# One ring of six PSUM banks for both kinds of attention scores, and another order of TensorE's work in each step

## The reference, cut to what matters

```
q = (x @ wq), k = (x @ wk), v = (x @ wv)          # split in heads
scores = einsum('bhqd,bhkd->bhqk', q, k) / sqrt(hd)
scores = where(causal, scores, min)
attn = softmax(scores, axis=-1)
ctx = einsum('bhqk,bhkd->bhqd', attn, v)
return ctx @ wo + bo
```

## Time and profile before

| | us |
|---|---|
| median of three runs (2633.34 to 2634.40) | 2634.18 |
| the profiled execution, its own time | 2634.95 |
| its span, first to last instruction | 2633.3 |
| attention, TensorE's first to last matmul in it (298.7 to 959.1) | 660 |
| PE busy / DVE / ACT / POOL over the span | 2435.7 / 1221.1 / 818.4 / 903.7 |

### The profile page before, as it was taken

One profiled execution on the slowest core, in us unless ns is written; L12 is line 12 of the kernel. 1 busy time (PEld: TensorE's weight loads), 2 busy tenths in 40 slices (PEclk: granted clock), 3 DMA queues, 4 the chain that ended last, 5 costly groups with the idle time before them and its releaser, 6 DMA issues. The chain is left out here.

```text
span 2633.3 us, 39827 instructions
## 1 busy us (share of the span) xinstructions
PE 2435.7 (92%) x12833; PEld 1800.0 (68%) x12833; DVE 1221.1 (46%) x2498; ACT 818.4 (31%) x1371; POOL 903.7 (34%) x1092
## 2 busy tenths in 40 slices
PE   7999699999999968599999996899999979999997
PEld 5888455555555536478888885688888768888886
DVE  3333477777777749701211113767766371111121
ACT  3222055555555541044444442101101112222221
POOL 0000155555555535323333333516243122222211
PEclk9999699999999988899999998899999989999999
DMA  6665735455445335410101102221312051000000
GB/s 246 225 223 193 182 84 135 108 120 132 108 120 132 77 111 176 157 40 17 64 32 63 62 19 84 96 94 66 110 49 96 31 191 40 32 32 32 32 33 32
DMA packets 154489, 255.29 MB, mean 97 GB/s; under 512 B 9648, under 2 KB 47536, under 8 KB 153904
## 3 DMA queue, kind: packets, MB, share of 16 engines
q1 hardware_dynamic: 137712, 208.20, 26.5%
q0 software_dynamic: 6144, 25.17, 2.9%
q10 hardware_dynamic: 10560, 20.97, 2.3%
HBM read 161.50 MB, written 92.27 MB: 96 GB/s over the span
## 5 line engine op out<-in xcount | busy, mean ns | idle before, releaser
L737 DVE CUSTOM_DVE_ANT_0 p_junk<-psum,p_causal 128x896 bf16<-128x896 f32 (+7 forms) x512 | 370.6, 752 | 159.8 <-PE psum L597 149.8
L700 ACT ACTIVATE p_probs<-psum 128x512 f32<-128x512 f32 (+1 forms) x640 | 331.3, 554 | 325.9 <-PE psum L608 320.6
L1149 POOL TENSOR_TENSOR p_h_lo<-p_h,p_h_hi 128x512 fp32r<-128x512 f32 x128 | 165.1, 1290 | 338.3 <-ACT p_h_hi L1178 338.3
L608 PE MATMUL psum<-p_qst,p_kst 98*128 98x512 f32 (+3 forms) x768 | 246.0, 384 | 17.2 <-ACT p_probs L700 10.9
L608 PEld LDWEIGHTS psum<-p_qst,p_kst 98*128 98x128 f32 x768 | 131.4, 190 | 170.8 <-ACT p_probs L700 84.8
L520 POOL TENSOR_SCALAR_AFFINE_SELECT p_probs<-p_probs 128x128 f32<-128x128 f32 x512 | 146.0, 306 | 264.8 <-ACT p_probs L700 263.8
L597 PE MATMUL psum<-p_kst,p_qst 96*128 96x512 f32 (+5 forms) x768 | 205.8, 369 | 20.8 <-DMA p_kst<-k_parts 17.3
L1802 POOL CAST p_h<-p_h 128x512 fp32r<-128x512 f16 x128 | 92.6, 723 | 373.1 <-ACT p_h L1826 373.1
L846 PE MATMUL psum<-p_xT_hi,tern 128*128 128x512 f32 x512 | 206.4, 403 | 1.4 <-DVE p_xT_lo L1248 1.4
L1217 PE MATMUL psum<-tern,p_h_hi 128*128 128x512 f32 x512 | 203.0, 397 | 2.1 <-POOL p_h_lo L1149 2.1
L846 PE MATMUL psum<-p_xT,p_w_hi 128*128 128x512 f32 x512 | 204.0, 398 | 0.7 <-ACT p_xT L1813 0.7
(11 more groups left out here) (184 smaller groups left out, 4639.8 us busy)
## 6 DMA issues: line engine op xcount, KB each, us to landing
p_qst<-q_parts SPq DMA_DIRECT2D x96, 256.0 KB, 4.5
p_kst<-k_parts SPq DMA_DIRECT2D x96, 256.0 KB, 6.8
q_parts<-p_qk_out SPq DMA_DIRECT2D x32, 512.0 KB, 2.8
k_parts<-p_qk_out SPq DMA_DIRECT2D x32, 512.0 KB, 2.7
ffn_x<-x SPq DMA_DIRECT2D x12, 1024.0 KB, 5.6
p_x<-in_x_t POOLq DMA_DIRECT2D x8, 1024.0 KB, 6.4
p_raw<-in_f_w POOLq DMA_DIRECT2D x8, 1024.0 KB, 8.0
v_rows<-p_v_out SPq DMA_DIRECT2D x32, 256.0 KB, 4.9
```

The lines of the kernel that those rows point to most:

```text
L608: mm = pe.matmul(ST_BANKS[st % 2][:, col:col + CH - q0], kst[s][0:KD + 2, g, j * P:(j + 1) * P], qst[s][0:KD + 2, c, g, q0:CH], start=True ...
L700: act.activation(probs[:, n % 2, g, col:CH], ST_BANKS[st % 2][:, col:CH], ACT.Exp, scale=SM_SCALE).then_inc(p_ready, 1)
L737: dve.tensor_tensor_reduce(halves_of(junk[:, which, 0:n]), scores, halves_of(causal[:, SEQ - n:SEQ]), 1.0, FLOOR, ALU.add, ALU.max, rowmax ...
L1149: pool.tensor_tensor(h_lo[:, m % 2, :], h[:, m % 2, :], f32(h_hi[:, m % 2, :]), ALU.subtract).then_inc(hl_done, 1)
```

## The change

All second and first scores take their banks from one ring of six (banks 0 to 5) in the order in which TensorE computes them. A long entry takes two adjoining banks (one is skipped at the ring's end). Each access waits for whoever used its bank last: for the exponential (`p_ready`) if that was a second score, for the maximum (`s_used`) if it was an entry. The ring is computed once for all units (`ring`), and the program checks that every unit of the same parity sees the same pattern. In the last unit, whose entries are left out, their banks stay reserved in the count, but nobody waits for them. The words of `STEPS` change as well. Two start values of semaphores are set by GpSimd where the semaphore is made and no longer by VectorE.

```diff
-    STEPS = [([(0, 0)], "seeesseeevose"), ([(0, 1), (0, 3)], "eesseseesvo"), ([(0, 2)], "sseeseseevoe"),
-             ([(1, 0)], "ssesesvo"), ([(1, 1)], "seesvosesee"), ([(1, 2)], "ssvsso"), ([(1, 3)], "sessesevo"),
-             ([(1, 4)], "sseessvo"), ([(1, 5), (1, 7)], "sseessvo"), ([(1, 6)], "sseessvo")]
+    STEPS = [([(0, 0)], "seseeseeeeseevo"), ([(0, 1), (0, 3)], "sesessevo"),
+             ([(0, 2)], "eeesssvos"), ([(1, 0)], "esesssevo"),
+             ([(1, 1)], "ssesveseo"), ([(1, 2)], "sssveeseo"),
+             ([(1, 3)], "sseessvo"), ([(1, 4)], "sesseveseo"),
+             ([(1, 5), (1, 7)], "ssessevo"), ([(1, 6)], "ssessevo")]
...
-        S_RING = 4
-        ST_BANKS = [psum[:, 4, :], psum[:, 5, :]]
...
+        N_BANKS = 6
...
         def ring():
...
+            taken, user, at = {}, {}, 0
+
+            def take(key, n):
+                nonlocal at
+                at += n == 2 and at % N_BANKS == N_BANKS - 1
+                taken[key] = [((at + k) % N_BANKS, user.get((at + k) % N_BANKS)) for k in range(n)]
+                at += n
+
+            def used(key):
+                for bank, _ in taken[key]:
+                    user[bank] = key
...
+            for u in range(NU):
+                at += -at % N_BANKS if u % 2 == 0 else 0
+                k = head = 0
+                for _, order in STEPS:
+                    for what in order:
+                        if what == "s":
+                            take(("s", u, head), 1)
+                            used(("s", u, head))
+                            head += 1
+                        elif what == "e":
+                            take(("e", u, k), n_banks(ROUND[k]))
+                            if u < NU - 1 or k == turned(1):
+                                used(("e", u, k))
+                            k += 1
+            return taken
...
+                def before(u, s, kind, n):
...
+                        if who == "e":
+                            out.append((bank, s_used, S_RING + (m if not steady and unit < 0 else LEAD + PER_ROUND * v + (0 if not steady and unit == NU - 1 else m)) + 1))
+                        else:
+                            out.append((bank, p_ready, 2 + ST_PER_UNIT * v + m + 1))
+                    return out
...
-                    for half, (bank, back) in enumerate(banks):
+                    for half, (bank, free, value) in enumerate(banks):
                         k0 = half * keys
-                        pe.wait_ge(s_used, S_RING + at - back + 1)
+                        if free is not None:
+                            pe.wait_ge(free, value)
...
-                    pe.wait_ge(p_ready, ST_PER_UNIT * u + st + 1)
+                    (bank, free, value), = before(u, s, "s", st)
+                    pe.wait_ge(free, value)
                     for c, j, q0, col in blocks_of(n):
-                        mm = pe.matmul(ST_BANKS[st % 2][:, col:col + CH - q0], kst[s][0:KD + 2, g, j * P:(j + 1) * P],
+                        mm = pe.matmul(psum[:, bank, col:col + CH - q0], kst[s][0:KD + 2, g, j * P:(j + 1) * P],
```

More of the change, by code:

```diff
@@ new lines, in used @@
+            def used(key):
+                for bank, _ in taken[key]:
+                    user[bank] = key
+            for k, e in enumerate(FIRST_ROUND):
+                take(("e", -1, k), n_banks(e))
+                used(("e", -1, k))
+            for u in range(NU):
[12 more added lines that the diff above has]
+                            k += 1
@@ new lines, in ring, with seen_from @@
+            return taken
+        RING = ring()
+        def seen_from(u, kind, n):
+            return [(bank, prev and (prev[0], prev[1] - u, prev[2])) for bank, prev in RING[kind, u, n]]
+        for u in range(NU - 2):
+            for n in range(ST_PER_UNIT):
+                assert (u == 0 and n < HPG) or seen_from(u, "s", n) == seen_from(2 + u % 2, "s", n)
+            for k in range(PER_ROUND):
+                assert (u == 0 and k < STEPS[0][1].count("e")) or seen_from(u, "e", k) == seen_from(2 + u % 2, "e", k)
@@ L434, in phase_attention, with banks_of @@
+        def banks_of(s, kind, n):
+            return [bank for bank, _ in RING[kind, 2 + s, n]]
         entries_in = lambda text: text.count("e")
@@ L581, in _, with score_entry @@
             def _(pe):
-                def score_entry(at, banks, e, u, s):
+                def before(u, s, kind, n):
+                    steady = not isinstance(u, int)
+                    out = []
+                    for bank, prev in RING[kind, 2 + s if steady else u, n]:
+                        if prev is None:
+                            out.append((bank, None, 0))
+                            continue
+                        who, unit, m = prev
+                        v = u + (unit - 2 - s) if steady else unit
+                        if who == "e":
[3 more added lines that the diff above has]
+                    return out
+                def score_entry(banks, e, u, s):
                     ahead, c, tile, g = e
@@ L586, in score_entry @@
                     if tile is None:
-                        (bank, back), = banks
-                        pe.wait_ge(s_used, S_RING + at - back + 1)
+                        (bank, free, value), = banks
+                        pe.wait_ge(free, value)
                         pe.wait_ge(nm_ready, 2 * (u + ahead) + c + 1)
@@ L706, in body @@
                     steps = pair_steps(i, last)
-                    for n, (u, _, step) in enumerate(steps[:2 * N_STEPS]):
+                    for n, (u, s, step) in enumerate(steps[:2 * N_STEPS]):
                         if n + 1 < len(steps):
@@ L775, in normalize_between @@
                         if part < PARTS - 1:
-                            entries(around, first + part, first + part + 1)
+                            entries(around, s, first + part, first + part + 1)
                 for k, e in enumerate(FIRST_ROUND):
-                    maximum(k, lead_banks[k], k % 2, e, -1)
-                entries(0, 0, TO[1])
+                    maximum(k, [bank for bank, _ in RING["e", -1, k]], k % 2, e, -1)
+                entries(0, 0, 0, TO[1])
                 def body(i, last):
```

48 lines of the change are left out of this document (21 added, 27 removed).

## The result

| | us |
|---|---|
| before, median (2633.34 to 2635.98) | 2634.29 |
| after, median of 4 runs (2612.50 to 2615.57) | 2614.65 |
| after, 5 more runs (2613.12 to 2615.77) | 2614.20 |
| ratio to before, 95% interval | 0.9924 [0.9906, 0.9941] |

What follows compares the result with a forecast made beforehand. It took attention to be bound by TensorE, with waits mostly on banks ScalarE still reads. 2634.95 - 14 (units) - 7.5 (last unit) = 2613.5; the median is 0.8 lower, so 2613 us, 80% range 2590 to 2641.

Steps and rivals of the forecast that it cites:

- Waits of a unit: In each attention unit on TensorE: waits fall from 2.9 to 1.3 us; with splits, 15 x 0.95 = 14 us less.
- splits: Steps where `v` and `o` are parted: 0.3 us a split, three instead of one, +0.6 us a unit, +10 us.
- Step 0: First step of a unit: an entry and the transpose wait for second scores' banks, 0.7 us in all.
- the small waits in the other steps: Outside steps 0 and 6: no bank waits but no room; some 0.5 us of small excesses beside short matmuls.
- Step 6: Its first second score waits for VectorE's maximum behind the product: 0.6 us taken, between 0.3 and 0.75.
- the product would end with GpSimd's first tensor-tensor: VectorE's product before step 6: by the shared-port rule it ends with that operation, wait 0.3 us, total 2609.
- The last unit: Attention's unit without entries: of 9.3 us of waits about 1.1 stay, two splits cost 0.6, so 7.5 us less.
- The head: Start of attention: the load of the turned maxima sets the first second score; 0 taken, with -1.5 to +1.
- The second scores wait for VectorE: Rival: the product stands over GpSimd's second tensor-tensor, step 6 waits 2.3 us more a unit; 2647, slower; chance 0.13.
- the clock stays what it is: TensorE in attention: its clock is unchanged, since nothing lets it idle; no time given to it.
- As many waits as before: Rival: waits move to VectorE's queue in place of ScalarE's, only the last unit gains; 2636, no change; chance 0.12.
- The maxima for c = 1: Rival: their load lands late for step 3, by 0.7 us in every unit; 2623; chance 0.08.

Runs made afterwards that it cites:

- v_o_together: The changed kernel with `v` and `o` side by side in steps 4, 5 and 7, same entries in each step: 2637.58 us.
- product_first: The changed kernel, but GpSimd starts ternarize's first tensor-tensor only when the product of half c = 0 is done: 2614.18 us.
- product_late: The changed kernel with three extra VectorE transposes, 2.1 us in all, just ahead of the product of half c = 0: 2667.54 us.
- after_again: The changed kernel itself, run again as a yardstick: 2614.20 us.
- before_max_first: The kernel before, with the load of the first turned maxima issued earlier in the head, as in max_first: 2633.20 us.
- ring_old_words: The changed kernel's common ring of six with the words of the kernel before: 2664.89 us.
- words_old_banks: The kernel before with the new words alone, its banks unchanged (four for entries, two for second scores): 2705.77 us.
- max_first: The changed kernel; SyncE issues the first turned maxima's load ahead of v of unit 0 and unit 1's last loads: 2608.83 us.

## Why the prediction was right, and where it was not

*Waits of a unit.* I had 2.9 before and 1.3 after, and 0.6 for splits, which I wrote as -0.95 though it adds up to -1.0 (0.7 us over 15 units). Measured: -0.93. Waits with all small excesses went from 3.6 to 2.1, 1.5 less where I had 1.6 less; v_o_together gives 0.3 a split. Step 0 was 0.7, and measured 0.8, in the entries behind the first second scores and at the transpose, as I said. That the sum comes so close is in part luck: step 6 has 0.3 us less than I gave it, and the small waits in the other steps, 1.0 us together where I had 0.5, take that back.

*Step 6* was wrong in its cause and its size. I had 0.6, for VectorE's maximum behind the product. It is 0.3, and it is for ScalarE: the third and fourth second score come back to the banks of the first two. I had seen that for the last unit, where the reserved entries fill the same four banks, and not for the others. product_first shows that the product's end, even 1.2 us earlier, changes nothing. That the product would end with GpSimd's first tensor-tensor was right: 0.54 after it, where I had 0.6. It lasts 0.69 alone (product_first), 1.87 in after and 2.19 in product_late, in the last two ending 0.54 behind GpSimd's. The Trainium skill's rule on the shared port (SBUF — State Buffer, Who interferes with whom) agrees. The 0.54 are less than the 0.69 that the product takes alone; no run shows why.

*The last unit.* -7.5 was predicted, -6.3 measured, and 0.4 more in the interval before it. Waits in it went from 8.6 to 1.9. The 1.04 of step 6 are as said (1.1); what I left out are 0.8 us of small waits in steps 1, 2, 3 and 8, where short second scores come with no entries between them. Counted from the unit's first second score, as in the prediction, it is 37.3 before and 31.4 after, -5.9: that stretch also holds 0.9 us at the transpose of step 0 (906.41, 908.15), which I had put at nothing. With the entries left out it comes to the bank of the second `s` before its exponential is done.

*The head.* 0 was right, and for the reason given: the load. VectorE did finish the head's maxima 5.3 us earlier (the last operation behind them starts at 321.97, before at 327.27; counted from the first entry it is 4.4), and the load took all of it: the first second score comes 28.8 us after the first entry in both. With the load out of the way attention is 5.3 us shorter than in after_again (635.12, 640.42), and without the ring (before_max_first) 0.5 shorter than in before (659.23, 659.77).

*The rivals.* "The second scores wait for VectorE" did not occur in after, but its margin was real: product_late moves VectorE by 2.1 us and makes it. Its price per unit (2.3 us, 34 in all) was too low, 53. In units without a fall of the clock it is 2.2 or 2.9, near the 2.3; the falls, which I had not in it, add some 13 us by the estimate above. I had written that the clock stays what it is; that held for after (1.00 from 340 to 900) and not for this rival. "As many waits as before" is what ring_old_words shows, and worse. The maxima for c = 1 weren't late: no second score of step 3 waits.

*What was not in the sum.* I took the change as two terms of about one size, a ring that ends waits and words that cost splits. The experiments show a product of two: the ring alone costs 30 us. The walk through banks had this in it, since it took the ring and the words together; the terms would have misled.

## What to carry to other kernels

A common ring of buffers for two consumers is only as good as the order in which its users come: walk the order through the ring bank by bank, with the durations of the trace, and don't price the ring and the order apart. When an engine gets faster somewhere, look for the transfer behind it in a queue: here one load, moved ahead in SyncE's order, gave 5.4 us more with the ring and at most 0.6 without it. And read waits in distances between starts on the engine that bounds; a table by releaser grew from 87.5 to 126 us while the waits shrank.

## What the runs showed of the hardware

In 9 of the units 1 to 13 of product_late TensorE's granted clock fell to 0.50, in a stretch in which it was otherwise busy: for 6.8 us in the unit shown (646.3 to 653.1), for 3.4 us in the others. Six of the falls came behind step 6's wait of 2.06 us, one behind 1.3 there, and two in step 3, where the nearest wait was one of 0.6 at the end of step 2. A unit with such a fall was 0.7 to 3.0 us longer than one without. The same wait of 2.06 in unit 1 had none. The waits of at most 0.9 us in after left the clock at 1.00 (340 to 900), and so did the 1.2 us of words_old_banks from 340 to 600. So the length of the last wait does not decide it alone, and no run shows what does. words_old_banks had one fall of 3.4 us too, in step 0 of one unit, with no wait over 0.6 us in the 10 us before it; that unit took 45.7 and not 44.2:

```profile
730.00:735.00 5.00, 4.86 (x29) 3.25 (x28) 3.27 (x13) 2.93 (x5) 1.24 (x5) 0.66 0.77 152
```

In the head of the attention TensorE runs at 1.2 GHz in every run. Between entries and second scores it stood idle for 7.0 us in after and for 2.3 in max_first; from the first second score to the rise of the clock it was then 9.9 us in the one and 8.4 in the other.

GpSimd's second tensor-tensor takes 2.61 in after, where it begins while the product is still pending (618.85, the product ends at 619.21), and 2.40 in before and in product_first, where none is. So the hold-up goes both ways, though GpSimd lost only 0.2.

The issue of the two loads of turned maxima kept SyncE for 10.28 us where it stood behind all loads of the first two units, and for 1.24 where it stood ahead of the last of them.
